# A dual attention kernel: the second batch's rotations ahead of the first score, and the first attention's operands in 64-row halves

## The chip, the cores and the metric

The kernel runs on one core of one Trainium2 chip. A core has a matrix engine (TensorE, PE in the profile; its weight loads are PEld), a vector engine (VectorE, DVE), a scalar engine (ScalarE, ACT), a general engine (GpSimd, POOL) and a queue engine that issues the transfers (SyncE, SP). The metric is the time of one execution on the device, in microseconds; lower is better.

## What is computed

Two sequences of 1024 tokens of width 128 are normalised. The result is the input plus a causal attention plus a small graph of attentions:

```python
xn = layernorm(x)                                  # x: (2, 1024, 128)
# first attention ("A"): 16 heads of width 8, rotated, causal
q, k, v = split(xn @ qkv_w.T + qkv_b)
q, k = apply_rope(q, cos, sin), apply_rope(k, cos, sin)
a = softmax(where(causal, -max, q @ k.T / sqrt(8))) @ v @ out_w.T + out_b
# second attention ("B"): six nodes c, 8 heads of width 16 each, no mask
q = ew[c,0] * (nodes[in_q] @ We[eq] + be[eq])      # k, v alike
nodes[c] = act_w[c] * mha(q, k, v, Wq[c], Wk[c], Wv[c], Wo[c]) + q
out = x + a + layernorm(nodes[5])
```

So there are 32 heads of the first attention (16 for each sequence) and 96 of the second.

## The kernel before

**The work of a head.** A head of either attention has two score products. The first (queries as rows, into the PSUM tiles `s1`, two of 1024 columns) serves only to find each query's largest score, which VectorE takes. GpSimd splits the negated maxima into three bf16 parts (`mparts`), TensorE transposes them into `misc`, ScalarE copies them to `mrows`, and a DMA puts them as three more rows under the queries (`qs`). The second product (keys as rows, into `s2`, two tiles of 512 columns) then has scores less maxima; ScalarE takes the exponential into `probs`, and TensorE multiplies with the values (`vs`) into `cps`. Scores are exact to float32, because queries and keys are split into bf16 parts that DRAM holds as six groups of rows: 6 x 8 = 48 rows in the first attention, 6 x 16 = 96 in the second.

**Operands.** There is a ring of four buffers `qs0..3` and `ks0..3`, 128 rows by 1024. A head of the first attention fills 48 of 96 rows, and the rest are zeros written at the start. The rows 96 to 98 hold the maxima in `qs` and ones in `ks`. First scores read 96 rows, second scores 99. A head's slot is `k % 4`.

**Strips.** Every score product and values' product is cut in four matmuls of 32 output rows each, at `tile_position=(0, c0)` with c0 = 0, 32, 64, 96 (`mm_strips`, and `context` for the values). On the diagonal a product of an identity with `mask_k` adds the causal mask.

**Order.** The work runs in phases of eight heads: `A0`, two of `AL`, `AZ` (the first attention), `B0`, ten of `BL`, `BE` (the second) and a tail `T`. A phase has eight steps k; step k does the first scores of head k, the second scores of head k-2 and the last of head k-3. A step of the first attention has five turns, in each of which TensorE does, in this order: a piece of second scores of head k-2 (up to 512 columns) and its mask; the first scores of head k (1024 columns, 512 in the last turn); the other piece; the values' product of the turn before; in turn 1 the transpose of the maxima; and side work named in a table (`START_AT` for A0, `PREP_A_AT` for AZ). SyncE issues in its own order: the loads of the next head, the raw context of head k-3, the maxima of head k-1, and where there are any the parts of the next operands. In step 7 the loads stand just ahead of the maxima.

**The rotations.** Queries and keys of the first attention come from `rotate` (a 512-column float32 product at full width on TensorE) and `turn` (two products with cosine and sine on VectorE, and for each pair a sum into `full`). ScalarE casts the high part (`high_part`), GpSimd subtracts it (`rest`), ScalarE casts the middle part (`middle_part`), GpSimd subtracts again (`low_part`), and SyncE writes the three parts to DRAM (`write_a`). Rotations 0 to 7 are the first sequence, ahead of the first score; 8 to 15, the second sequence, are side work of the phase A0, at the places marked "rot" in `START_AT`. Between the two stand weight products (`products`, read by ScalarE), the values of the first sequence and 18 one-column bias products (`biases(0)`).

## Time and profile before

| | us |
|---|---|
| median of 3 runs | 1427.39 (1426.09 to 1428.78) |
| the profiled execution | 1423.05 |
| its span | 1421.3 |
| 38.6 to 104.5: phase A0 | 65.9 |
| 104.5 to 208.9: the two phases AL | 104.4 |
| 208.9 to 268.1: phase AZ | 59.2 |
| 268.1 to 1367.7: the second attention | 1099.6 |
| 1367.7 to the end | 53.6 |

A row of a timeline gives start and duration in us, the engine, the line of the program, the operation, the tiles written and read, the shapes (96*32 is 96 rows by 32 columns of weights), the count, and in brackets the idle time before it with what ended it. Rows of one kind that follow each other are merged. A matmul's duration includes its way through the array, so a row's end lies after the start of the next; lengths of TensorE's work are read from start to start. A float32 product counts as two passes.

### The profile page before, as it was taken

What the parts mean: (1) busy time and instruction counts of PE and PEld (TensorE: products, weight loads), DVE (VectorE), ACT (ScalarE), POOL (GpSimd) and SP (SyncE); (2) the same over time, 40 slices, a digit from 0 to 9 for tenths busy, and PEclk for the clock granted to TensorE, in tenths of its full rate; (3) what the DMA queues carried; (4) which work ended last, traced back from release to release, by engine and by line L of the source; (5) the groups of instructions that cost most, each with busy time, mean ns of one, the idle gap of its engine ahead of it and who ended that gap; (6) DMA issues with size and microseconds to landing.
All of it is one profiled execution on the core that took longest, in us unless ns stands there. A gap on an engine that the chain in (4) does not pass through costs nothing.

```text
span 1421.3 us, 60282 instructions
## 1 busy us (share of the span) xinstructions
PE 1380.5 (97%) x26216; PEld 935.3 (66%) x26216; DVE 1263.0 (89%) x1587; ACT 1139.5 (80%) x2133; POOL 449.8 (32%) x936
## 2 busy tenths in 40 slices
PE   6899999999999999999999999999999999999995
PEld 4467777656667666676676766766667666667652
DVE  8889999999989989899899898988989989989895
ACT  3378887688878878888788887887888878878784
POOL 5141115324422433233423332234233432330210
PEclk9899999999999999999999999999999999999998
DMA  8131112343232422333323323233233332321211
GB/s 253 47 116 60 51 59 98 119 142 119 81 127 70 132 97 77 102 109 107 104 78 114 107 74 121 83 123 107 69 101 107 101 107 80 127 98 56 76 38 40
DMA packets 115668, 137.68 MB, mean 97 GB/s; under 512 B 14972, under 2 KB 90109, under 8 KB 115277
## 3 DMA queue, kind: packets, MB, share of 16 engines
q1 hardware_dynamic: 115405, 133.83, 28.7%
q8 instruction: 207, 3.39, 1.0%
q14 instruction: 56, 0.46, 0.1%
HBM read 64.63 MB, written 61.98 MB: 89 GB/s over the span
## 4 chain that ended last, share of the span: by engine, by line
PE 88%; DMA 4%; DVE 3%; SPq 2%; ACT 1%; POOL 1%; issue 1%; ACTq 0%; POOLq 0%; DVEq 0%
PE s L1069 53%; PE cps L1163 26%; PE misc L1069 7%; DMA qs<-mrows 2%; DVE neg_max L971 1%; SPq L431 1%; PE misc L1064 1%; ACT probs L784 1%; DMA dram_raw_b<-csb 1%; PE s L1064 0%; DVE s L967 0%; POOL parts L601 0%; POOL ks L596 0%; POOL full L614 0%; SPq L500 0%
## 5 line engine op out<-in xcount | busy, mean ns | idle before, releaser
L784 ACT ACTIVATE probs<-s 128x512 f32<-128x512 f32 x1792 | 1059.2, 599 | 227.4 <-PE s L1069 166.8
L971 DVE TENSOR_REDUCE neg_max<-s 128x1 f32<-128x1024 f32 x768 | 936.5, 1222 | 62.0 <-PE s L1069 9.1
L1069 PE MATMUL s<-qs,ks 99*32 99x512 bf16 (+2 forms) x7680 | 808.4, 370 | 7.1 <-DMA qs<-mrows 5.1
L1069 PE MATMUL s<-ks,qs 96*32 96x512 bf16 (+2 forms) x7680 | 606.5, 369 | 6.3 <-DMA ks<-dram_qk_a 2.7
L1163 PE MATMUL cps<-probs,vs 128*32 128x256 f32 (+1 forms) x7552 | 591.4, 368 | 0.6 <-ACT probs L784 0.6
L1069 PEld LDWEIGHTS s<-qs,ks 99*32 99x32 bf16 x7680 | 235.8, 94 | 240.6 <-ACT probs L784 96.7
L1163 PEld LDWEIGHTS cps<-probs,vs 128*32 128x32 f32 x7552 | 316.4, 110 | 76.3 <-issue 17.0
L1069 PEld LDWEIGHTS s<-ks,qs 96*32 96x32 bf16 x7680 | 292.5, 97 | 88.6 <-issue 24.5
L633 POOL TENSOR_TENSOR mparts<-neg_max,zeros 128x8 bf16<-128x8 f32 x128 | 26.0, 203 | 796.0 <-DVE neg_max L971 654.3
L967 DVE CUSTOM_DVE_ANT_0 s<-s,mask_q 128x1024 f32<-128x1024 f32 (+7 forms) x256 | 187.8, 785 | 23.5 <-PE s L1069 14.8
L706 POOL TENSOR_TENSOR parts<-full,zeros 128x512 bf16<-128x512 f32 x48 | 61.4, 1280 | 52.2 <-DVE full L949 52.2
L1069 PE MATMUL misc<-srcT,cur 128*32 128x512 f32 x544 | 74.1, 592 | 0.0
L1069 PE MATMUL s<-mask_k,ident_h 128*32 128x128 bf16 x1024 | 65.4, 221 | 0.0
L710 POOL TENSOR_TENSOR parts<-full,zeros 128x512 bf16<-128x512 f32 x48 | 61.4, 1279 | 3.8
L712 POOL TENSOR_TENSOR parts<-full,parts 128x512 bf16<-128x512 f32 x48 | 56.0, 1167 | 3.8
L708 POOL TENSOR_TENSOR full<-full,parts 128x512 f32<-128x512 f32 x48 | 55.9, 1165 | 3.8
L949 DVE TENSOR_SCALAR full<-misc,cur_bias 128x512 f32<-128x512 f32 x48 | 36.0, 750 | 14.0 <-PE misc L1069 12.3
L793 ACT COPY csb<-cps 128x256 f32<-128x256 f32 x128 | 46.9, 367 | 0.8 <-PE cps L1163 0.8
L772 ACT COPY mrows<-misc 24x128 bf16<-24x128 bf16 x128 | 32.4, 253 | 13.3 <-PE misc L1336 13.3
L1069 PEld LDWEIGHTS s<-mask_k,ident_h 128*32 128x32 bf16 x1024 | 33.7, 97 | 4.3 <-issue 1.8
L967 DVE DVE_READ_ACCUMULATOR2_ANT neg_max<- 128x1 f32 x256 | 36.0, 141 | 0.0
L944 DVE TENSOR_SCALAR srcT<-misc,cur_bias 128x512 f32<-128x512 f32 x20 | 15.0, 750 | 23.4 <-PE misc L1069 23.4
(134 smaller groups left out, 607.6 us busy)
## 6 DMA issues: line engine op xcount, KB each, us to landing
dram_qk_b<-parts SPq DMA_DIRECT2D x48, 384.0 KB, 3.2
qs<-dram_qk_b SPq DMA_DIRECT2D x96, 192.0 KB
ks<-dram_qk_b SPq DMA_DIRECT2D x96, 192.0 KB
dram_qk_b<-parts SPq DMA_DIRECT2D x48, 256.0 KB, 3.2
dram_raw_b<-csb SPq DMA_DIRECT2D x93, 128.0 KB, 4.3
dram_qk_b<-parts SPq DMA_DIRECT2D x48, 128.0 KB, 3.2
vsrc<-srcT SPq DMA_DIRECT2D x12, 512.0 KB, 3.1
ctx_b<-dram_raw_b SPq DMA_DIRECT2D x44, 128.0 KB
```

What stands on the lines that cost most here:

```text
L706: pl.tensor_tensor(p[:, 0, :], f[:, :], zeros[:, :], ALU.add).then_inc(parts_done, 1)
L708: pl.tensor_tensor(f[:, :], f[:, :], p[:, 0, :], ALU.subtract).then_inc(parts_done, 1)
L710: pl.tensor_tensor(p[:, 1, :], f[:, :], zeros[:, :], ALU.add).then_inc(parts_done, 1)
L712: pl.tensor_tensor(p[:, 2, :], f[:, :], p[:, 1, :], ALU.subtract).then_inc(parts_done, 1)
L772: nc.scalar.copy(mrows[(k - 1) % 2][:, :], misc_rows).then_inc(mrow_sb, 1)
L784: nc.scalar.activation(buf[:, lo:hi], s2[bank][:, 0:hi - lo], ACT.Exp, scale=scale).then_inc(exp_done, 1)
L793: nc.scalar.copy(csb[(k - 3) % 2][:, :], cps[:, 0:GQ]).then_inc(ctx_sb, 1)
L949: ve.tensor_scalar(full[(2 * (what == "q") + w) % STAGES][:, :], misc[:, :], cur_bias[:, op:op + 1], None, ALU.add).then_inc(prep_full, 1)
L967: last = ve.tensor_tensor_reduce(out=scores, in0=scores, in1=mask_q[:, S - hi + lo:S], scale=-1.0, scalar=-MASKED, op0=ALU.add, op1=ALU.mi ...
L971: last = ve.tensor_reduce(peak, scores, AX.X, ALU.max, negate=True)
L1069: last = te.matmul(dst[c0:c0 + STRIP, :], lhsT[:, c0:c0 + STRIP], rhs, start=start, stop=stop, tile_position=(0, c0))
L1163: last = te.matmul(cps[g * VW:(g + 1) * VW, GQ - 128 * len(mine):GQ], vs[k % RING][:, j, :], blocks[:, first:first + (len(mine) - 1) * ste ...
```

## The change

The rotations 8 to 15 move from the phase A0 to the stretch ahead of the first score. So do their casts on ScalarE; GpSimd's part follows in steps 0 and 1 of A0. The twelve scalings of output and edge weights move from VectorE to ScalarE. The 18 bias products move the other way, behind first scores, in three pieces ("edge"). The side work left in A0 moves to earlier or other turns.

The operands of the first attention lie in two buffers `qa0`, `qa1` (new) and two `ka0`, `ka1` (in the space of `ctx_b`, named so below). Head k uses buffer k % 2, in rows 0 to 63 or 64 to 127 by k % 4 // 2: 48 rows of data and the three rows of maxima or ones behind them. The matmuls of both score products get `tile_position=(row, c0)` with row 0 or 64. The mask is cut to 64 rows too; where a strip's keys lie in the other half, a shifted mask (`mask_far`) stands for `mask_k`. Zero rows are no longer written; GpSimd writes the ones of the second attention's `ks` ahead of its first power. In step 7 of AZ the maxima go ahead of the loads.

```diff
-            (0, 4): ("rot", 8), (1, 2): ("rot", 9), (1, 4): ("rot", 10), (2, 2): ("rot", 11),
...
+START_AT = {(0, 0): ("edge", 0), (0, 1): ("edge", 1), (0, 2): ("edge", 2), (1, 2): ("bias", 1), (1, 4): ("bias", 2),
+            (2, 2): ("bias", 3), (2, 4): ("va", 2), (3, 2): ("va", 3)}
...
+        def first_row(which, k):
+            return HALF_ROWS * (k % RING // 2) if which == "A" else 0
+        def operands(which, k):
+            return (qa[k % 2], ka[k % 2]) if which == "A" else (qs[k % RING], ks[k % RING])
+        def data_rows(which, k):
+            row = first_row(which, k)
+            return slice(row, row + (ROWS_A if which == "A" else KROW))
+        def score_rows(which, k):
+            row = first_row(which, k)
+            return slice(row, row + (ROWS_A if which == "A" else KROW) + 3)
...
-                    if k == UP - 1 and kind not in ("BE", "T"):
+                    if k == UP - 1 and kind not in ("AZ", "BE", "T"):
                         load_unit(kind, r, UP, b)
...
+                    if kind == "AZ" and k == UP - 1:
+                        load_unit(kind, r, UP, b)
...
-                    if kind == "A0" and 2 <= k < 2 + 2 * NCH:
-                        n = 2 * NCH + k - 2
-                        rest(n)
-                        low_part(n)
+                    if kind == "A0" and k == 0:
+                        rest(2 * NCH)
+                        for n in range(2 * NCH + 1, 4 * NCH):
+                            rest(n)
+                            if n < 4 * NCH - 1:
+                                low_part(n - 1)
+                    if kind == "A0" and k == 1:
+                        low_part(4 * NCH - 2)
+                        low_part(4 * NCH - 1)
...
+            for n in range(2 * NCH, 4 * NCH):
+                for h in range(2):
+                    turn(2 * n + h, (s2[0], s2[1], cps, misc)[(2 * n + h) % 4])
...
+            def mask_strips(dst, row):
+                rows = slice(row, row + HALF_ROWS)
+                for c0 in range(0, 128, STRIP):
+                    here = c0 // HALF_ROWS == row // HALF_ROWS
+                    at, mask = (c0, mask_k) if here else ((c0 + HALF_ROWS) % 128, mask_far[row // HALF_ROWS])
+                    last = te.matmul(dst[c0:c0 + STRIP, :], ident_h[rows, at:at + STRIP], mask[rows, :],
+                                     start=False, stop=True, tile_position=(row, c0))
...
-                    last = mm_strips(bank[:, first - lo:end - lo], ky[0:KALL, t * 128:(t + 1) * 128],
-                                     q[0:KALL, q0 + first - at:q0 + end - at], stop=not diagonal)
+                    last = mm_strips(bank[:, first - lo:end - lo], ky[rows, t * 128:(t + 1) * 128],
+                                     q[rows, q0 + first - at:q0 + end - at], stop=not diagonal, row=row)
                     if diagonal:
-                        last = mm_strips(bank[:, at - lo:at - lo + 128], ident_h[:, :], mask_k[:, :],
-                                         start=False)
+                        last = mask_strips(bank[:, at - lo:at - lo + 128], row)
```

TensorE, the end of the stretch ahead of the first score, before (`srcT,w_a` 128x512 is a rotation, `s_0<-srcT` and `s_1<-srcT` are weight products, `be_sb` the bias products, `ks,qs` the first scores):

```order
L1064 MATMUL misc<-be_sb,srcT 128x1 [waits rot_done]
L1064 MATMUL misc<-be_sb,srcT 128x1 x17
L1064 MATMUL s_1<-srcT 128x128 [waits va_sb]
L1064 MATMUL s_1<-srcT 128x128 x2
L1064 MATMUL s_1<-srcT 128x128 [waits va_sb]
L1064 MATMUL s_1<-srcT 128x128 x2
L1064 MATMUL s_0<-srcT 128x128 [waits comp_sb,va_sb]
L1064 MATMUL s_0<-srcT 128x128 x2
L1064 MATMUL s_0<-srcT 128x128 [waits comp_sb,va_sb]
L1064 MATMUL s_0<-srcT 128x128 x2
L1069 MATMUL s_0<-ks,qs 32x512 [waits qk_in0,pool_const,comp_sb]
```

TensorE, the same place now:

```order
L1106 MATMUL s_0<-srcT,w_a 128x512 [waits rot_done,xt_sb]
L1106 MATMUL s_1<-srcT 128x128 [waits va_sb]
L1106 MATMUL s_1<-srcT 128x128 x2
L1106 MATMUL s_1<-srcT,w_a 128x512 [waits rot_done,xt_sb]
L1106 MATMUL s_1<-srcT 128x128 [waits va_sb]
L1106 MATMUL s_1<-srcT 128x128 x2
L1106 MATMUL cps<-srcT,w_a 128x512 [waits rot_done,xt_sb]
L1106 MATMUL s_0<-srcT 128x128 [waits comp_sb,va_sb]
L1106 MATMUL s_0<-srcT 128x128 x2
L1106 MATMUL misc<-srcT,w_a 128x512 [waits rot_done,xt_sb]
L1106 MATMUL s_0<-srcT 128x128 [waits comp_sb,va_sb]
L1106 MATMUL s_0<-srcT 128x128 x2
```

The last four of the eight rotations now stand between the weight products, and the bias products are gone from here.

GpSimd, from the first head's values (`vs`) on, before (L633 to L639 split the maxima of head 0; L614 is `rest`, L601 `low_part`):

```order
L653 COPY vs<-vtok_a 128x8x8 [waits va_sb]
L633 TENSOR_TENSOR mparts<-neg_max,zeros 128x8 [waits max_done]
L635 TENSOR_TENSOR mres<-neg_max,mparts 128x8 [waits max_parts]
L637 TENSOR_TENSOR mparts<-mres,zeros 128x8 [waits max_parts]
L639 TENSOR_TENSOR mparts<-mres,mparts 128x8 [waits max_parts]
L653 COPY vs<-vtok_a 128x8x8
```

GpSimd, the same place now (L647 is `rest`, L634 `low_part`, L666 the first of the split):

```order
L686 COPY vs<-vtok_a 128x8x8 [waits va_sb]
L647 TENSOR_TENSOR full<-full,parts 128x512 [waits rope_hi] x2
L634 TENSOR_TENSOR parts<-full,parts 128x512 [waits rope_mid]
L647 TENSOR_TENSOR full<-full,parts 128x512 [waits rope_hi]
L634 TENSOR_TENSOR parts<-full,parts 128x512 [waits rope_mid]
L647 TENSOR_TENSOR full<-full,parts 128x512 [waits rope_hi]
L666 TENSOR_TENSOR mparts<-neg_max,zeros 128x8 [waits max_done]
```

Six operations of the second sequence now stand ahead of the split of head 0's maxima.

SyncE, the last step of AZ, before (`csb` is the raw context, `mrows` the maxima, `dram_qk_b` the second attention's first operands):

```order
L500 DMA dram_raw_a<-csb0 128x256 [waits ctx_sb]
L431 DMA qs0<-dram_qk_b 96x1x1024 [waits written]
L431 DMA ks0<-dram_qk_b 96x1x1024
L520 DMA qs2<-mrows0 3x8x128 [waits mrow_sb]
L431 DMA qs1<-dram_qk_b 96x1x1024 [waits pv_done]
```

SyncE, the same place now:

```order
L525 DMA dram_raw_a<-csb0 128x256 [waits ctx_sb]
L546 DMA qa0<-mrows0 3x8x128 [waits mrow_sb]
L456 DMA qs0<-dram_qk_b 96x1x1024 [waits written]
L456 DMA ks0<-dram_qk_b 96x1x1024
L456 DMA qs1<-dram_qk_b 96x1x1024 [waits pv_done]
```

The maxima changed places with the two loads.

## Rows read from the trace of the kernel before

**Rows 1.** The page, part 1: busy us, share of the span and instructions by engine.

```profile
PE 1380.5 (97%) x26216; PEld 935.3 (66%) x26216; DVE 1263.0 (89%) x1587; ACT 1139.5 (80%) x2133; POOL 449.8 (32%) x936
```

**Rows 2.** Windows by stage; columns: stretch, length, busy us by engine, TensorE clock, DMA.

```profile
38.60:104.50 65.90, 62.77 (x1239) 38.15 (x1243) 56.64 (x143) 37.73 (x77) 21.80 (x49) 0.92 0.25 82
104.50:208.90 104.40, 104.30 (x2904) 79.76 (x2900) 96.75 (x256) 89.88 (x177) 15.48 (x79) 1.00 0.18 55
208.90:268.10 59.20, 57.50 (x1552) 42.99 (x1548) 52.54 (x135) 44.93 (x89) 28.09 (x60) 1.00 0.34 114
268.10:287.70 19.60, 18.58 (x419) 10.69 (x414) 19.54 (x18) 11.72 (x23) 5.94 (x9) 1.00 0.30 97
```

**Rows 3.** Timeline, VectorE: first tile of heads 1 and 3; columns: start, us, instruction, idle before.

```profile
38.65 1.23 DVE L967 CUSTOM_DVE_ANT_0 s<-s,mask_q 128x1024 f32<-128x1024 f32 x1 [6.11 <-PE s L1069]
...
56.62 1.22 DVE L967 CUSTOM_DVE_ANT_0 s<-s,mask_q 128x1024 f32<-128x1024 f32 x1
```

**Rows 4.** Timeline, TensorE, the head that begins on it at 155.75 us.

```profile
155.75 0.40 PE L1069 MATMUL s<-qs,ks 99*32 99x512 bf16 x4
...
158.40 0.44 PE L1069 MATMUL s<-qs,ks 99*32 99x512 bf16 x4
...
158.68 0.66 PE L1069 MATMUL s<-ks,qs 96*32 96x512 bf16 x12
...
159.40 0.66 PE L1163 MATMUL cps<-probs,vs 128*32 128x256 f32 x10
159.82 0.44 PE L1069 MATMUL s<-qs,ks 99*32 99x512 bf16 x4
...
162.22 0.41 PE L1069 MATMUL s<-qs,ks 99*32 99x512 bf16 x4
```

**Rows 5.** Timeline, VectorE, the same head, first tile at 156.80 us.

```profile
156.80 1.23 DVE L967 CUSTOM_DVE_ANT_0 s<-s,mask_q 128x1024 f32<-128x1024 f32 x1 [0.69 <-POOL mres L635]
...
159.40 0.97 DVE L967 CUSTOM_DVE_ANT_0 s<-s,mask_q 128x768 f32<-128x768 f32 x1
...
162.74 0.14 DVE L967 DVE_READ_ACCUMULATOR2_ANT neg_max<- 128x1 f32 x1
```

**Rows 6.** Timeline, SyncE, then the chain of 150 to 157 us: DMAs of row maxima.

```profile
159.20 0.77 SPq L520 DMA_DIRECT2D qs<-mrows  x1
...
153.12 2.58 DMA qs<-mrows
```

**Rows 7.** Timeline, TensorE: two passes at full width, two in strips, and what follows each.

```profile
59.41 1.12 PE L1064 MATMUL misc<-srcT,w_a 128*128 128x512 f32 x2
60.47 0.40 PE L1069 MATMUL s<-qs,ks 99*32 99x512 bf16 x4
...
1385.52 1.03 PE L1069 MATMUL s<-srcT,comp 128*32 128x512 f32 x8
1386.38 0.39 PE L1069 MATMUL s<-qs,ks 99*32 99x512 bf16 x4
```

**Rows 8.** Timeline, TensorE, around one transpose.

```profile
709.60 0.39 PE L1069 MATMUL s<-qs,ks 99*32 99x512 bf16 x3
709.65 0.22 PE L1336 MATMUL misc<-ident_h,mparts 128*24 128x128 bf16 x1
```

**Rows 9.** Timeline, TensorE, at the end of the first attention.

```profile
267.07 0.40 PE L1069 MATMUL s<-qs,ks 99*32 99x512 bf16 x4 [1.70 <-DMA qs<-mrows]
```

**Rows 10.** Groups by line, 38.6 to 104.5 us: the rotations in the first phase.

```profile
L864 DVE SCALAR_TENSOR_TENSOR rope<-misc,bias_a,table 128x512 f32<-128x512 f32 x8 | 6.0, 748 | 1.1 <-PE misc L1064 0.7
...
L870 DVE TENSOR_TENSOR full<-rope 128x512 f32<-128x512 f32 x4 | 2.8, 694 | 0.1
```

**Rows 11.** Timeline, prologue: GpSimd, TensorE, ScalarE.

```profile
15.39 3.98 POOL L596 MEMSET ks<- 32x1024 bf16 x4
...
26.17 4.08 PE L1064 MATMUL misc<-be_sb,srcT 128*128 128x1 f32 x36
...
35.22 0.88 ACT L741 ACTIVATE comp<-s,ewb 128x128 f32<-128x128 f32 x3 [0.35 <-PE s L1064]
```

More of the change, by code:

```diff
@@ L1106, in _ @@
             pe.wait_ge(wqk_in, 16)
-            for m in range(4 * NCH):
+            for m in range(8 * NCH):
                 pe.wait_ge(xt_sb, m // 4 + 1)
@@ L1277, in score_piece @@
                 which = kind_at(kind, k, 2)
-                q, ky = qs[(k - 2) % RING], ks[(k - 2) % RING]
+                q, ky = operands(which, k - 2)
+                rows, row = score_rows(which, k - 2), first_row(which, k - 2)
                 lo, hi = pieces(which, j)[n]
```

141 lines of the change are left out of this document (78 added, 63 removed).

## The prediction

> **What bounds the kernel now.** I read the page first: TensorE is busy for 97% of the span, VectorE for 89% [rows 1]. The busy time by stage comes next: the first attention fills three windows (its first phase, two phases without side work, a last phase that also prepares the second attention), 229.5 us of 1421.3, and only these windows are touched by the change, with the prologue ahead of them [rows 2]. In the middle window TensorE is busy for 104.30 of 104.40 us and VectorE for 96.75. The windows begin where VectorE takes a head's first 1024-wide tile: head 1 at 38.65, head 3 at 56.62 [rows 3], head 9 at 104.5. The 16 heads of the middle window take 6.52 us each, and eight heads cost 65.9 us in the first window and 59.2 in the last.
>
> One head on TensorE, start to start [rows 4]: a turn begins with one score piece and its diagonal mask, 0.28 (158.40 to 158.68); the tile's first scores and the second piece with its mask take 0.72, the probabilities times values 0.42, together 1.42. By columns (512, 128; 1024; 512, 128) the 1.00 of scores is 0.22 + 0.06, 0.44, and 0.22 + 0.06. Three such turns leave 2.2 us of the head's 6.47 (155.75 to 162.22) for the shorter first and last. Nothing is idle, so **TensorE is the bound**. VectorE is close behind: its last read of a head starts 5.94 us after its first tile, with no gap marked before the tiles but for short waits on the next scores, two a head, as before the tile at 159.40 [rows 5]. I estimate 0.3 us for them from the starts and durations, and 5.65 us for a head without them. A third loop runs through SyncE: the DMA that brings the row maxima back is issued 2.40 us after the head's first tile (159.20 against 156.80 [rows 5, 6]), lands about 2.6 us later, and TensorE needs 0.8 to 1.1 us from there to the next head's first tile (some 0.7 us of scores and 0.36 until VectorE starts). That loop is 5.8 to 6.1 us. So a faster TensorE can bring a head from 6.5 to about 5.9, not further.
>
> **Part 1: half-height operands.** Both score products of the first attention go from 96 and 99 rows to 48 and 51, in rows 0 to 63 or 64 to 127. Head k's first scores and head k-2's second scores always lie in opposite halves. The count of matmuls and columns is unchanged: a mask is still one per strip. The height alone buys nothing: 99-row and 96-row pieces take their 0.22 us for 512 columns alike [rows 4].
>
> What it can buy is overlap of the halves. Per turn the second scores are 0.22 + 0.06 + 0.22 + 0.06 = 0.56 and the first 0.44; side by side they take 0.56 instead of 1.00. No row shows two halves at work. The nearest is the column strips: four matmuls of 512 columns cost 0.22, the price of one. And strips do not wait for each other: the transpose is ahead of the next scores in the program and uses the first strip only; it starts at 709.65, while three of the four scores behind it had started at 709.60 [rows 8]. One strip was late and the others passed it. I take it that the halves behave alike.
>
> What it costs: the values' product keeps all 128 rows, so the array's division changes twice a turn, ten times a head. No row shows 64 against 128 rows. The nearest change is 32-column strips to full width: two passes of 512 columns cost 0.86 in strips (1385.52 to 1386.38) and 1.06 at full width between strips (59.41 to 60.47) [rows 7]. That is 0.20 for two changes, 0.10 each, with whatever part of it is weight loading. Bounds 0 and 0.2; I take 0.10, the measured one.
> The Trainium skill, page "TensorEngine Tiling (Array Packing)", section "Key Properties", says that changing the tiling mode drains the engine, and that different tiles can run in parallel. The first speaks against this change and agrees with the 0.10; the second no run here shows.
>
> TensorE per head follows. Full overlap: three turns 0.56 + 0.42 + 0.20 = 1.18, first turn about 1.0, last turn 0.28 + 0.42 + 0.20 = 0.90, sum **5.45**. If starts keep program order over the halves, the second piece can begin only when the first scores' last group has begun: a turn is 0.22 + 0.22 + 0.28 + 0.42 + 0.20 = 1.34, the head **6.2 to 6.3**. No overlap at all: 6.47 + 10 x 0.10 = **7.5**. The page "TensorE: Matmul & The Clock Gate", section "The mechanism", of the Trainium skill has matmuls start and end strictly in program order; rows 8 disagree for strips, and by that rule the time would be the middle value's.
>
> Middle window, full overlap: VectorE and the maxima loop set 5.9. The eighth head of a phase has its loads ahead of the maxima DMA (the one of 153.12 in rows 6, by my estimate 0.7 us later in its head than the other), which keeps 6.5. 14 x 5.9 + 2 x 6.5 = 95.6 against 104.4: **-8.8**. In program order 14 x 6.35 + 2 x 6.8 = 102.5: -1.9. Serial 16 x 7.5 = 120: +15.6.
>
> Last window (59.2 us): four heads carry one projection, two strip passes, together 0.86 on TensorE as in rows 7, and SyncE's writes; I put them at 6.7 against some 7.35, the seventh with two at 7.3. In the eighth the maxima DMA now goes ahead of the loads for the second attention. Before, it went behind them, and TensorE sat 1.70 us for it until 267.07 [rows 9]. Now it lands early, but the loads start about 1.4 us later and the first tile of the second attention waits for them: I put this head at 9.2 against 8.3. Sum 5.9 x 2 + 6.7 x 4 + 7.3 + 9.2 = 55.1: **-4.1**. In program order about 0, serial +8.
>
> Where the first two heads of the second attention share turns with the last two of the first, each turn of the old kind now changes the division up to four times: 2 x 18 x 0.10 = 3.6 us on TensorE. In that stretch VectorE is busy for 19.54 of 19.60 us and TensorE for 18.58 [rows 2], so about 1 us of the 3.6 is covered. Some more is in turns without a piece of the first attention. I take **+2.0**; bounds 0 and 3.6.
>
> **Part 2: the second batch's rotations.** Before, eight of them sit in the first phase: eight products on TensorE, 8 x 0.748 + 4 x 0.694 = 8.8 us on VectorE [rows 10]. Each stands in a turn at full width (1.06 us with its two changes [rows 7]). Now they stand ahead of the first score. What hides them there: TensorE spent 4.08 us on 36 passes of one-column bias products (now behind the first scores in three pieces); VectorE sat idle 6.11 us before the first tile [rows 3, 11]. The way of the operands to DRAM and back is not longer, since GpSimd's four memsets (3.98 us), which held its first subtraction until 19.4, now stand ahead of its first power [rows 11]. But TensorE gets 8 x 0.86 = 6.9 us [rows 7] less 4.1: up to +2.8 on its way to the last weight product, which ScalarE copied out by 36.1 [rows 11]. The first score waits for that copy as for its operands, and had 1.8 us of room. I leave the first tile at 38.6, bounds 37 and 40.5.
>
> Behind it stands the cost of the move. ScalarE now does 12 activations taken from VectorE (0.29 each by the three of 0.88 us in rows 11, 3.5 us), then eight casts; GpSimd does rest, rest, low, rest, low, rest, six of about 1.2 us, in program order **ahead of** head 0's maxima, and TensorE's transpose waits for these. From 38 + 3.5 + 0.6: 42.1 + 7.0 = 49.1, split maxima at about 50, transposed and copied at 50.6, DMA to 53.2 [rows 6], the third head's first tile not before 54.3; I take 54.8 against 56.62: **-1.8**. Heads 3 to 8 took 47.9 us. They lose five rotations, keep two value products and one bias, and keep SyncE's write of three parts behind each load: 7.2 + 6.9 + 3 x 6.8 + 6.7 = 41.2: **-6.7**. In program order 42.5, serial 47.7.
>
> **Sum.** -1.8 - 6.7 - 8.8 - 4.1 + 2.0 = -19.4. The profiled execution took 1423.05 us (span 1421.3), the median is 1427.39, 4.3 above it. I carry the difference over: 1427.4 - 19.4 = **1408.0**.
>
> **Rivals.**
> Starts in program order across the halves: -1.8 - 5.4 - 1.9 + 0 + 2.0 = -7.1, 1420. For it: no row shows halves; against it: rows 8.
> The halves do not run side by side and each division change costs 0.10: -1.8 - 0.2 + 15.6 + 8 + 2.0 = +23.6, **1451**, slower. It decides where the values' product meets the scores, ten times a head. With some 30 heads and 6 to 8 us from part 2, the kernel is slower once TensorE's head goes above about 6.7 us, that is when overlap saves less than 0.8 of the 1.0 us that the changes cost. Against it: strips show that parts of the array work side by side.
> Overlap works but a change costs about 0.2: TensorE's head is 6.5 and only part 2 is left: about 1423.
> The rotations are only displaced (the first tile comes at 41, the third head later still): 1408 + 5 = 1413; inside the range.
>
> **How the numbers follow.** Full overlap (with the displaced rotations) 0.52, program order 0.22, dear changes 0.10, serial 0.16. The forecast is the first. The range reaches from 1398 (loop at 5.65, first tile at 37) to 1429 and leaves the serial case out. A measurement here tells 0.2% (2.9 us) from no change. Faster: 0.52 + 0.22 + half of dear = 0.78; same 0.04; slower 0.18.
>
> **What would show it.** Middle window 104.4 to about 96 us with VectorE busy near its whole length; first and second scores with starts inside each other's 0.2 us; ten gaps of 0.1 us a head around the values' product; third head's first tile near 55; the window from 287.7 to 1367.7 (the second attention after its first heads) unchanged in length. A middle window of 120 us would prove me wrong on overlap, one of 102 on order, and a first tile after 41 on the prologue.

## The result: slower by 0.5% where 1.4% faster was forecast

| kernel | median, us | lowest to highest | runs |
|---|---|---|---|
| before | 1428.40 | 1426.09 to 1431.25 | 10 |
| after | 1434.27 | 1432.96 to 1441.12 | 10 |

The ratio is 1.0054, 95% interval 1.0042 to 1.0066: 6 to 9 us lost. The forecast was 1408.0 in a range of 1398 to 1429, so even the range missed. The profiled execution of the changed kernel has a span of 1431.6 us against 1421.3. Times and ratios here are of executions whose mean granted clock is 0.97 or more; two of the four of x4, at 0.87, took 1627 and 1635 us and stand in none of them.

The page, part 1 and the granted TensorE clock by slice:

```profile
PE 1385.3 (97%) x26216; PEld 878.2 (61%) x26216; DVE 1256.8 (88%) x1569; ACT 1136.3 (79%) x2145; POOL 450.9 (31%) x940
...
PEclk9699999799999999999999999999999999999998
```

Beside [rows 1] no share of a working engine has moved by more than a point; only the weight loads fell, from 66% to 61%. So the page's first part does not show where the time went. The clock line does: the second slice (36 to 72 us) and the eighth (251 to 286 us) stand at 6 and 7, where the page of the kernel before has 8 and 9. The windows by stage, to be laid beside [rows 2]; columns: stretch, length, busy us by engine, clock, DMA share, GB/s:

```profile
36.70:57.80 21.10, 18.97 (x170) 12.02 (x173) 13.86 (x37) 7.50 (x19) 10.39 (x16) 0.54 0.06 21
57.80:104.20 46.40, 44.21 (x1104) 22.48 (x1088) 36.41 (x98) 32.56 (x67) 11.04 (x34) 0.88 0.32 107
104.20:206.60 102.40, 98.41 (x2904) 50.53 (x2896) 94.65 (x256) 84.58 (x177) 16.02 (x83) 1.00 0.19 56
206.60:265.50 58.90, 54.41 (x1544) 27.72 (x1536) 51.65 (x134) 42.63 (x89) 27.49 (x57) 0.98 0.35 115
265.50:282.40 16.90, 16.90 (x205) 5.60 (x204) 9.75 (x9) 6.00 (x11) 0.00 (x0) 0.55 0.10 32
282.40:294.30 11.90, 11.56 (x222) 4.88 (x221) 10.69 (x11) 5.90 (x12) 5.90 (x9) 1.00 0.35 113
```

| stretch | before | after | forecast change | measured change |
|---|---|---|---|---|
| to the third head's first tile | 56.62 | 57.80 | -1.8 | +1.2 |
| heads 3 to 8 | 47.9 | 46.4 | -6.7 | -1.5 |
| middle window, 16 heads | 104.4 | 102.4 | -8.8 | -2.0 |
| last window, 8 heads | 59.2 | 58.9 | -4.1 | -0.3 |
| first two heads of the second attention | 19.6 | 28.8 | +2.0 | +9.2 |

Together +6.6. The other 3.7 us of the longer span lie behind them, in heads whose instructions are the same: from VectorE's first tile of the third of these heads to its last they took 1089.1 us before and 1093.2 after, and 1089.1 to 1098.5 over the profiles of this study, whatever had been changed. I take that stretch for one execution's scatter: the profiled execution was 5.4 us faster than its kernel's median before, and 0.8 after. From here on kernels are compared by the time at which that third head begins (287.7 before, 294.3 after), and by the ratio of their runs. The first of these measures scatters too. Four kernels that are the same up to the eighth head of the last phase (after, x1, x2, x14) begin it at 253.9 to 255.8 us, so less than 2 us there says nothing.

Where the +9.2 comes from stands in the timeline of TensorE, VectorE and SyncE at the end of the first attention; columns: start, us, instruction, and in brackets the idle time ahead of it:

```profile
257.64 0.76 SPq L546 DMA_DIRECT2D qa<-mrows  x1
258.44 0.81 SPq L456 DMA_DIRECT2D qs<-dram_qk_b  x1
259.29 0.75 SPq L456 DMA_DIRECT2D ks<-dram_qk_b  x1
...
264.34 1.04 PE L1111 MATMUL s<-ks,qs 96*32 96x512 bf16 x8 [3.04 <-DMA ks<-dram_qk_b]
...
265.51 1.22 DVE L1013 TENSOR_REDUCE neg_max<-s 128x1 f32<-128x1024 f32 x1 [4.24 <-PE s L1111]
```

The chain of waits has this load in it; columns: start, us, what:

```profile
259.29 5.01 DMA ks<-dram_qk_b
```

The load of the second attention's operands is issued behind the maxima DMA and TensorE stands idle for 3.04 us. But the stall is not the loss. Eight 512-column strips take 1.04 us behind it, where the same group took 0.60 to 0.65 from 284 us on: the clock is at its lower level of 1.2 GHz, as the windows show, and stays there for 17 us:

```profile
262.00:264.00 2.00, 0.00 (x0) 0.00 (x0) 0.00 (x0) 0.01 (x1) 0.54 (x3) 0.91 0.29 103
264.00:268.00 4.00, 3.66 (x40) 0.97 (x44) 1.82 (x2) 0.97 (x2) 0.00 (x0) 0.50 0.00 0
...
276.00:280.00 4.00, 4.00 (x56) 1.64 (x51) 1.55 (x3) 1.44 (x3) 0.00 (x0) 0.50 0.00 0
280.00:284.00 4.00, 4.00 (x63) 1.46 (x55) 3.84 (x4) 1.46 (x3) 1.04 (x5) 0.91 0.02 4
```

Before the change TensorE sat idle for 1.70 us at the same place [rows 9] and the clock stayed at 1.00.

Side by side work did come. Start times in one turn of the middle window:

```profile
150.43 0.40 PE L1111 MATMUL s<-qa,ctx_b 51*32 51x512 bf16 x4
150.46 0.40 PE L1111 MATMUL s<-ctx_b,qa 48*32 48x512 bf16 x4
...
150.69 0.28 PE L1111 MATMUL s<-ctx_b,qa 48*32 48x256 bf16 x4
150.72 0.28 PE L1111 MATMUL s<-qa,ctx_b 51*32 51x256 bf16 x4
150.80 0.28 PE L1111 MATMUL s<-ctx_b,qa 48*32 48x256 bf16 x4
...
151.09 0.36 PEld L1218 LDWEIGHTS cps<-probs,vs 128*32 128x32 f32 x10 [0.16 <-issue]
151.66 0.10 PEld L1111 LDWEIGHTS s<-qa,ctx_b 51*32 51x32 bf16 x4 [0.21 <-ACT probs L835]
```

A second score (51 rows) and a first score (48 rows) start 0.03 us apart and the next matmuls of each half follow 0.23 us later; and the second piece (150.72) starts ahead of a first score that stands before it in the program (150.80). Weight loads stand still for 0.16 us ahead of the values' product, where they wait for nothing that the profile shows, and for 0.21 us ahead of the next score, which the profile puts down to ScalarE.

### The profile page after: what moved, and what is told of

Same layout as the page of the kernel before. It is cut to its first block, busy times and chain, and to the rows that moved or that the text cites. A ratio compares the mean times of both kernels' runs of the same rounds, so it can differ in the third digit from the quotient of the medians.

```text
span 1431.6 us, 60283 instructions
## 1 busy us (share of the span) xinstructions
PE 1385.3 (97%) x26216; PEld 878.2 (61%) x26216; DVE 1256.8 (88%) x1569; ACT 1136.3 (79%) x2145; POOL 450.9 (31%) x940
## 4 chain that ended last, share of the span: by engine, by line
PE 81%; DMA 8%; SPq 6%; ACT 2%; DVE 2%; issue 1%; POOL 0%; ACTq 0%; DVEq 0%
PE s L1111 46%; PE cps L1218 24%; PE misc L1111 7%; DMA qs<-mrows 3%; DMA dram_raw_b<-csb 2%; SPq L456 2%; ACT probs L835 2%; SPq L493 1%; PE misc L1106 1%; DMA qa<-mrows 1%; SPq L424 1%; PE s L1121 1%; DMA ctx_b<-dram_qk_a 1%; PE s L1106 1%; SPq L502 1%
## 5 line engine op out<-in xcount | busy, mean ns | idle before, releaser
L1111 PE MATMUL s<-qs,ks 99*32 99x512 bf16 x6144 | 684.9, 381 | 6.2 <-DMA qs<-mrows 4.3
L1111 PE MATMUL s<-ks,qs 96*32 96x512 bf16 x6144 | 512.0, 381 | 4.0 <-DMA ks<-dram_qk_b 3.0
L1111 PEld LDWEIGHTS s<-qs,ks 99*32 99x32 bf16 x6144 | 183.4, 93 | 218.9 <-ACT probs L835 88.2
L1111 PEld LDWEIGHTS s<-ks,qs 96*32 96x32 bf16 x6144 | 248.1, 98 | 65.0 <-issue 20.4
L666 POOL TENSOR_TENSOR mparts<-neg_max,zeros 128x8 bf16<-128x8 f32 x128 | 26.0, 203 | 815.8 <-DVE neg_max L1013 666.0
L1111 PE MATMUL s<-qa,ctx_b 51*32 51x512 bf16 (+3 forms) x1536 | 111.2, 341 | 6.4 <-ACT probs L835 4.4
L1111 PE MATMUL s<-ctx_b,qa 48*32 48x512 bf16 (+3 forms) x1536 | 96.2, 344 | 4.7 <-DMA ctx_b<-dram_qk_a 2.5
L1111 PEld LDWEIGHTS s<-qa,ctx_b 51*32 51x32 bf16 x1536 | 31.5, 91 | 66.5 <-ACT probs L835 42.6
L1121 PE MATMUL s<-mask_k,ident_h 64*32 64x128 bf16 x512 | 58.2, 224 | 0.0
L1121 PE MATMUL s<-mask_far,ident_h 64*32 64x128 bf16 x512 | 58.2, 224 | 0.0
```

The costliest lines, as they stand in the source:

```text
L1111: last = te.matmul(dst[c0:c0 + STRIP, :], lhsT[:, c0:c0 + STRIP], rhs, start=start, stop=stop, tile_position=(row, c0))
L1121: last = te.matmul(dst[c0:c0 + STRIP, :], ident_h[rows, at:at + STRIP], mask[rows, :], start=False, stop=True, tile_position=(row, c0))
```

## Experiments

All kernels below start from the changed kernel unless said otherwise. "Third head" is the time at which the third head of the second attention begins. Code cuts are shown in part; `...` marks what is left out.

| kernel | third head, us | median, us | ratio to before, 95% interval |
|---|---|---|---|
| before | 287.7 | 1428.4 | |
| after | 294.3 | 1434.3 | 1.0054, 1.0042 to 1.0066 |
| x1, loads first | 292.2 | 1431.8 | 1.0028, 1.0015 to 1.0041 |
| x2, seven products in the stall | 289.4 | 1429.8 | 1.0007, 0.9995 to 1.0019 |
| x3, rotations only | 287.5 | 1426.5 | 0.9990, 0.9978 to 1.0003 |
| x5, biases early | 295.1 | 1432.7 | 1.0033, 1.0021 to 1.0045 |
| x6, projections early | 297.8 | 1435.7 | 1.0049, 1.0032 to 1.0067 |
| x8, all three | 282.9 | 1422.0 | 0.9961, 0.9948 to 0.9974 |
| x11, x8 and 30 products | 285.3 | 1425.2 | 0.9993, 0.9981 to 1.0005 |
| x12, x8 at full height | 286.5 | 1424.9 | 0.9990, 0.9980 to 1.0000 |
| x13, full height, late loads | 288.9 | 1428.4 | 1.0013, 0.9998 to 1.0028 |
| x14, loads first, one product | 284.6 | 1422.3 | 0.9967, 0.9954 to 0.9980 |
| x15, x8 and 10 products | 290.1 | 1429.1 | 1.0015, 1.0001 to 1.0030 |
| x16, halves only | 293.6 | 1433.2 | 1.0050, 1.0038 to 1.0063 |

### x1: the loads first

```diff
-                    if k == UP - 1 and kind not in ("AZ", "BE", "T"):
+                    if k == UP - 1 and kind not in ("BE", "T"):
                         load_unit(kind, r, UP, b)
...
-                    if kind == "AZ" and k == UP - 1:
-                        load_unit(kind, r, UP, b)
```

> The changed kernel with one thing undone: in the eighth head of the last first-attention phase the loads for the second attention go ahead of the maxima DMA again. Theory 1 (the loads wait for a chain of fixed length: the last projection's parts are written at 253.6 us, land some 4.5 us later, and only then can the load of 5 us begin; the half clock follows from TensorE's idle time): the loads move by 0.8 us at most (258.44 to some 257.7), the maxima DMA goes 1.6 us later and lands behind them, TensorE is still idle for about 3 us, its clock is still halved, the second attention's first head stays at 15 to 17 us and the time within 1.5 us of 1434. Theory 2 (the order on SyncE alone is the cause, as my prediction had it with 9.2 us for that head): TensorE idle as before the change, 1.7 us, no half clock, first head 9 to 10 us, time 1424 to 1427. Theory 3 (four division changes a turn cost the 7 us): head at 16, time 1434 whatever the idle time.

The stall became 1.68 us, now for the maxima, as short as before the change. The clock fell all the same and the first head took 16.1 us. The gain of 2.1 us is that of the eighth head (8.4 us instead of 10.2) and of the first head (16.1 instead of 16.9), less some 0.5 us of scatter ahead of and behind them. Theory 2 falls, and so does the part of theory 1 that wanted 3 us of idle time. The fall is no accident of one execution: the mean granted clock is 0.978 to 0.982 in all twelve of x1 and 0.975 to 0.981 in all ten of the changed kernel, and 0.987 to 0.992 in those of the kernel before. Timeline of TensorE, then windows, of x1:

```profile
263.01 0.40 PE L1109 MATMUL s<-qa,ctx_b 51*32 51x512 bf16 x4 [1.68 <-DMA qa<-mrows]
```
```profile
264.00:268.00 4.00, 4.00 (x60) 1.16 (x56) 3.44 (x3) 1.97 (x5) 0.00 (x0) 0.60 0.21 53
268.00:272.00 4.00, 4.00 (x51) 1.51 (x47) 1.47 (x2) 1.46 (x3) 0.00 (x0) 0.50 0.23 82
```

### x2: products that keep TensorE busy

```diff
+                            if (kind, k, i) == ("B0", 0, 0):
+                                need(pe, mrow_sb, UP * ph - 1)
+                                for f in range(7):
+                                    mm(misc[:, :], w_a[:, f % 2 * D:(f % 2 + 1) * D], srcT[:, f % 2 * CH:(f % 2 + 1) * CH])
```

> The changed kernel with seven extra products of 512 columns (nobody reads their result), queued on TensorE between the last second scores' first piece and the first scores of the second attention, where it stood idle for 3.4 us. Theory 1 (the idle time brought the half clock, and the half clock made the second attention's first head 16.9 us long): the extra products fill some 3 us of the idle time, the granted clock stays at its full level from 264 us on, that head takes 9.1 to 10.5 us, the time falls by 6 to 8 us to 1426 to 1428. Theory 3 (division changes in mixed turns are the cost): the head stays above 14 us and the time at 1434 or more.

I had mis-sized them: each is two passes, and the 14 took 6.28 us, some 3 more than the stall. The time fell nevertheless, by 4.5 us (6 to 8 expected), because the clock stayed up. TensorE's timeline, and the windows of the two heads:

```profile
260.19 6.28 PE L1106 MATMUL misc<-srcT,w_a 128*128 128x512 f32 x14
```
```profile
267.10:277.50 10.40, 10.23 (x205) 4.10 (x201) 9.33 (x8) 5.89 (x11) 0.00 (x0) 1.00 0.17 53
277.50:289.40 11.90, 11.56 (x221) 4.88 (x221) 10.71 (x11) 5.89 (x11) 5.90 (x9) 1.00 0.35 113
```

10.4 and 11.9 us at full clock against 16.9 and 11.9, and 9.1 and 10.5 before: the half clock costs 6.5 us, the divided turns 2.7. Theory 3 holds for those 2.7 only.

### x3 and x16: each half of the change alone

x3 gives the operands their full height back, and puts the loads ahead of the maxima DMA again:

```diff
-            return (qa[k % 2], ka[k % 2]) if which == "A" else (qs[k % RING], ks[k % RING])
+            return qs[k % RING], ks[k % RING]
...
```

> Only the second half of the change: the second batch is rotated ahead of the first score, the operands of the first attention have the full height of before (96 and 99 rows) and the loads stand ahead of the maxima DMA as before. Theory A (the bias products, moved behind the first scores, stand in VectorE's way at half clock and eat what the earlier rotations give): third head's first tile at 57 to 58 us against 56.62, middle window 104.4, last window 59.2, second attention's first head 9.1, time within 2 us of before (1427 to 1430). Theory B (the rotations do give the 8.5 us that I predicted and the division changes at half clock took them again): window from the third head to the middle one 42 us, time 1419 to 1422.

Theory A: 0.9990, third head's first tile of the first attention at 58.3 (37.9 plus 11.5 and 8.8 us), middle heads 6.49, the second attention's first head 9.1. The early rotations alone give 0.1%, which the interval does not tell from nothing.

x16 has the half-height operands with rotations, biases and weight products as before:

```diff
+START_AT = {(0, 0): ("bias", 1), (0, 1): ("bias", 2), (0, 2): ("bias", 3),
+            (0, 4): ("rot", 8), (1, 2): ("rot", 9), (1, 4): ("rot", 10), (2, 2): ("rot", 11),
...
```

> Only the first half of the change: half-height operands, with the second batch's rotations, the bias products and the products of weights where they were before. With the rotations the clock should be back by 50 us as before; middle heads 6.31, last ones 7.06; the loads behind the maxima DMA give the stall of 3 us and the half clock where the second attention begins: 16.9 and 11.9 us for its first two heads. Sum against before: -3.0 in the middle, -2 in the last window, +7.8 +1.4 at the boundary, about +4: 1430 to 1433. If the early rotations were what made the changed kernel slower, it would be at or below 1428.

1.0050, the boundary (the place where the second attention begins) as in the changed kernel: stall 2.81 us, half clock, 17.0 and 12.0 us for the two heads. The loss belongs to the first part of the change. One expectation failed: the clock at the start was back at 61 us and not by 50, although the rotations stood in the turns again. In x3, without them and at full height, it was 61 us too.

### x4: the same half for both scores

```diff
-            return HALF_ROWS * (k % RING // 2) if which == "A" else 0
+            return 0
-            return (qa[k % 2], ka[k % 2]) if which == "A" else (qs[k % RING], ks[k % RING])
+            return qs[k % RING], ks[k % RING]
...
```

> The changed kernel with all operands of the first attention in rows 0 to 63 (48 and 51 rows, in eight tiles of their own), so that first and second scores can't run side by side while the division of the array still changes ten times a head. If the halves do overlap in the changed kernel and a change costs 0.10 us, a head of the middle window takes 7.3 to 7.5 us (against 6.31), the window 117 to 120 us (against 102.4), and the 32 heads together add 30 to 36 us: 1464 to 1470. If overlap brought nothing there (heads bound by order across the halves), the window would stay near 103 and the time near 1434.

A middle head takes 7.60 us, the kernel 1.0311 times the one before (1.0281 to 1.0341), some 1472 us. VectorE's first tiles of two such heads:

```profile
143.57 1.23 DVE L1009 CUSTOM_DVE_ANT_0 s<-s,mask_q 128x1024 f32<-128x1024 f32 x1 [0.74 <-PE s L1111]
151.17 1.23 DVE L1009 CUSTOM_DVE_ANT_0 s<-s,mask_q 128x1024 f32<-128x1024 f32 x1 [0.74 <-PE s L1111]
```

Against 6.50 at full height that is 1.10 for ten changes of the division, 0.11 each: my 0.10 was right, and so was the 7.5 for serial halves. Side by side work takes 1.3 us off a head.

### x7, x9, x10: what sets a middle head at 6.31 us

```diff
+                            skip = 128 if kind[0] == "A" and hi - lo > 128 else 0
+                            lo += skip
...
+                                hi -= 128 if kind == "AL" and hi - lo == CH else 0
```

x7 has the first two lines, on VectorE: it leaves the first 128 keys out of the maxima. x9 has the last one, on ScalarE: it leaves 128 columns of each long piece out of the exponentials, in the two middle phases. x10 has all three. Each was run once; what counts here is the length of a head.

> The changed kernel with VectorE's reads of the first attention's scores 128 columns shorter in all tiles wider than 128 (the first 128 keys are left out of the maxima), seven reads a head, some 0.13 us each: VectorE's work falls from 5.92 to some 5.0 us a head, TensorE's stays. If VectorE's own work and its hand-over of the tiles set the 6.31 us of a middle head, a head falls by 0.4 or more, to 5.9 or less, where the maxima loop takes over. If TensorE sets them (second scores held back by program order, the rival of 6.2 to 6.3), the head stays at 6.2 to 6.3.

> The changed kernel with ScalarE's exponentials 128 columns shorter in every piece of 512 columns in the two middle phases of the first attention (the last 128 columns of such a piece are left out and keep older values). ScalarE's work falls by some 0.13 us for each of its long pieces, VectorE's and TensorE's stay. Shorter VectorE reads alone had left the middle head at 6.31 us. If the round trip between TensorE and ScalarE sets the head (a piece's exponential ends, the product with the values and the next piece and mask follow on TensorE, then ScalarE starts again), the head falls to 5.8 to 6.2 us. If TensorE's own order across the halves sets it (the rival of my prediction), or VectorE and TensorE together, it stays within 0.05 of 6.31.

> Both cuts together: VectorE's reads 128 columns shorter in all of the first attention and ScalarE's exponentials 128 columns shorter in its two middle phases (those columns are left out). If two loops of nearly the same length (VectorE's tiles, and TensorE with ScalarE) each hold the head at 6.31 us, this falls clearly below what the shorter exponentials alone give: 5.5 to 5.9 us. If the TensorE-ScalarE loop alone sets it, it is the same as there. If TensorE's program order sets it: 6.2 to 6.3.

The same tile in two heads that follow each other, of x7, x9 and x10 in turn:

```profile
140.21 1.10 DVE L1011 CUSTOM_DVE_ANT_0 s<-s,mask_q 128x896 f32<-128x896 f32 x1 [0.56 <-POOL mres L668]
146.51 1.10 DVE L1011 CUSTOM_DVE_ANT_0 s<-s,mask_q 128x896 f32<-128x896 f32 x1 [0.56 <-POOL mres L668]
```
```profile
128.00 1.23 DVE L1010 CUSTOM_DVE_ANT_0 s<-s,mask_q 128x1024 f32<-128x1024 f32 x1 [0.27 <-PE s L1112]
134.09 1.23 DVE L1010 CUSTOM_DVE_ANT_0 s<-s,mask_q 128x1024 f32<-128x1024 f32 x1 [0.27 <-PE s L1112]
```
```profile
126.44 1.10 DVE L1012 CUSTOM_DVE_ANT_0 s<-s,mask_q 128x896 f32<-128x896 f32 x1 [0.56 <-POOL mres L668]
132.34 1.10 DVE L1012 CUSTOM_DVE_ANT_0 s<-s,mask_q 128x896 f32<-128x896 f32 x1 [0.56 <-POOL mres L668]
```

6.31 with less VectorE work, 6.10 with less ScalarE work, 5.90 with both. So the round trip of TensorE and ScalarE sets the head, VectorE's tiles stand 0.2 us behind it, and TensorE's program, which is the same in all three, needs 5.90 or less. What sets the 5.90 of x10 is open. The rival "program order, 6.2 to 6.3" had the right number for the wrong reason. The round trip in the changed kernel's ScalarE timeline, one head:

```profile
164.13 2.31 ACT L835 ACTIVATE probs<-s 128x512 f32<-128x512 f32 x4 [0.18 <-PE s L1121]
166.79 0.60 ACT L835 ACTIVATE rec_b<-s 128x512 f32<-128x512 f32 x1 [0.34 <-PE s L1121]
167.74 1.08 ACT L835 ACTIVATE probs<-s 128x512 f32<-128x512 f32 x2 [0.35 <-PE s L1121]
```

Four exponentials run without a gap, while TensorE waits for a bank that ScalarE has read; then TensorE's values' product stands ahead of the next piece and mask, and ScalarE waits 0.34 and 0.35 us. I take it that the two banks for the second scores are too few to cover both; no run has more of them.

### x5, x6, x8: the version that beats both

x5 takes the bias products back ahead of the first score; x6 moves the projections of the last window, and the writes of their parts, one head earlier:

```diff
-START_AT = {(0, 0): ("edge", 0), (0, 1): ("edge", 1), (0, 2): ("edge", 2), (1, 2): ("bias", 1), (1, 4): ("bias", 2),
+START_AT = {(1, 2): ("bias", 1), (1, 4): ("bias", 2),
...
-PREP_A_AT = {(2, 2): ("k", 0), (3, 2): ("k", 1), (4, 2): ("q", 0), (5, 2): ("q", 1),
+PREP_A_AT = {(1, 2): ("k", 0), (2, 2): ("k", 1), (3, 2): ("q", 0), (4, 2): ("q", 1),
...
```

> The changed kernel with the 18 bias products of one column back ahead of the first score (behind the weight products), and VectorE's sums of them too. In the changed kernel they stand in three pieces inside the first head and take 1.43, 2.65 and 2.66 us of TensorE at half clock, and VectorE waits behind each. If these pieces are what ate the gain of the early rotations, the first head takes 7 to 8 us instead of 12.3, the first score comes 1 to 2 us later, and everything up to the middle window comes 3 to 4 us earlier: time 1430 to 1431 against 1434. If the half clock of this stretch is the cause whatever is queued there, the heads behind take up the difference and the time stays within 1.5 us of 1434.

> The changed kernel with the four key and query projections of the last first-attention phase, and the writes of their parts, one head earlier; the loads for the second attention still behind the maxima DMA of the eighth head. Theory 1 (a chain of fixed length from the last projection to the loads sets the stall): the loads no longer wait for the write and are issued at once behind the maxima DMA, but that is the same place on SyncE, 258.4 us by the trace of the changed kernel, so the stall is shortened only by the time that the load itself takes less without the write's traffic (5.0 us to some 3 to 4): idle time 1.5 to 2.5 us, time 1430 to 1434. If the stall comes from the order on SyncE alone, nothing changes: 1434.

x5: first tile at 41.5, first head 6.4 us instead of 12.3: 1.1 us of gain by the end of the first head, 1.6 in the median, but no gain by the third head of the second attention (295.1 against 294.3), so no more than the 1.1 us is shown. Its own third head took 11.6 us at half clock against 9.0, which is not its doing: x1 and x2, the changed kernel up to there, took 12.35. x6: the stall is still 2.75 us (1.5 to 2.5 expected; the load takes 4.7 us with the write gone from beside it), the half clock lasts longer still, two slow heads instead of one (17.8 and 19.3 us): nothing won.

x8 has both, and issues the loads one head earlier, behind the seventh head's maxima DMA:

```diff
-                    if kind == "AZ" and k == UP - 1:
+                    if kind == "AZ" and k == UP - 2:
                         load_unit(kind, r, UP, b)
```

> The changed kernel with the bias products back ahead of the first score, the four projections one head earlier, and the loads for the second attention in the seventh head instead of the eighth, behind its maxima DMA. Then neither operands nor maxima are late where the second attention begins: TensorE idle under 1 us there, clock at its full level, first head of the second attention 10.4 us as with the filler, and 3 us less idle time than there: from the filler's 1429.8 less 3 us of overfilling, less up to 3 us of the biases: 1424 to 1427. If the half clock comes anyway, 1430 or more.

0.9961, better than the 1424 to 1427 us expected: TensorE shows no wait at the boundary, and the clock stays:

```profile
262.00:266.00 4.00, 4.00 (x83) 1.56 (x76) 3.41 (x4) 2.64 (x5) 0.00 (x0) 1.00 0.35 110
266.00:270.00 4.00, 3.88 (x86) 1.67 (x78) 3.55 (x4) 1.80 (x4) 0.00 (x0) 1.00 0.08 27
```

x12 is x8 with operands of full height, which need the loads back in the eighth head, ahead of its maxima DMA:

> The faster version (1422.0 us) with the first attention's operands at full height as before the change, and the loads for the second attention ahead of the maxima DMA in the eighth head, which full-height operands need. It tells what the half-height operands bring once the clock drop where the second attention begins is gone. By the heads: -0.19 us in each of 16 middle heads, -0.3 in each of the last seven, +2.7 us in the two mixed heads, and what a stall of 1.5 us at the boundary costs this one: half-height ahead by 2 to 5 us, this kernel at 1424 to 1427. If the half-height operands bring nothing on the whole: 1421 to 1423.

0.9990. So half height, with the earlier loads that it allows, brings 0.3% (4 us) once the clock stays up, 3.6 us of it by the third head: x8 reaches the second attention 6.2 us earlier (260.6 against 266.8), 1.5 of them a stall that x12 has and x8 has not, and loses 2.6 us in its first two heads (22.3 against 19.7).

### x13 and x14: idle time or kind of work

x13 is x3 with the loads behind the maxima DMA. x14 is x1 and one product of 512 columns, `mm(misc[:, :], w_a[:, 0:D], srcT[:, 0:CH])`, ahead of the wait for the maxima.

> Early rotations and full-height operands, but the loads for the second attention behind the eighth head's maxima DMA, as the changed kernel has them. Its twin with the loads first lost 1.47 us of TensorE there and kept the full clock. If the length of the idle time alone decides, TensorE is idle here for 2.5 to 4 us, the clock falls to half as in the changed kernel and the first head of the second attention takes 14 to 17 us: time 1432 to 1435. If full-height work leaves the clock up even after a stall of this length, the first head takes 9.1 us and only the stall is added: 1427 to 1429.

> The changed kernel with the loads ahead of the maxima DMA (there TensorE was idle for 1.68 us and the clock was halved all the same, 1431.8 us) and one extra product of 512 columns (two passes, 0.9 us, read by nobody) ahead of the wait for the maxima. If the idle time is what halves the clock at half-height operands too, 0.8 us of it leave the clock at its full level: first head of the second attention 10.4 us, second 11.9, time 1425 to 1428. If the clock falls for another reason (the light mixed turns that follow), the head stays at 16 us and the time at 1431 to 1432.

The stall and the clock behind it, x13 and then x14:

```profile
268.51 0.62 PE L1110 MATMUL s<-ks,qs 96*32 96x512 bf16 x8 [2.62 <-DMA ks<-dram_qk_b]
```
```profile
266.00:268.50 2.50, 0.00 (x0) 0.00 (x0) 0.07 (x2) 0.60 (x1) 1.03 (x5) 1.00 0.32 119
268.50:272.00 3.50, 3.23 (x76) 1.77 (x80) 2.75 (x3) 1.98 (x4) 0.00 (x0) 1.00 0.08 19
```
```profile
259.44 1.13 PE L1104 MATMUL misc<-srcT,w_a 128*128 128x512 f32 x2
261.14 0.40 PE L1109 MATMUL s<-qa,ctx_b 51*32 51x512 bf16 x4 [0.57 <-DMA qa<-mrows]
```
```profile
262.00:266.00 4.00, 4.00 (x77) 1.32 (x73) 3.48 (x3) 2.72 (x6) 0.00 (x0) 1.00 0.19 53
```

At full height 2.62 us of idle time leave the clock up. At half height 1.68 us halve it (x1) and 0.57 us, after one product at full width, don't. So the length of the stall doesn't decide alone; which of the two things that x14 has changed, less idle time or a product at full width, kept the clock up isn't separated. Every execution agrees: mean clock 0.986 to 0.988 in the ten of x13, 0.987 and 0.988 in the four of x14. One product of 1.1 us that nobody reads goes with 0.9967 instead of 1.0028, 8.7 us. Not all of that is its doing: the traces show 5.7 us in the first two heads (22.3 against 28.1), and 1.8 us that x14's profiled execution was ahead of x1's before it reached the product.

### x11 and x15: buying the clock back in the first heads

```diff
+                        if kind == "A0" and (k, i) in [(0, 0), (0, 1), (0, 2), (0, 3), (0, 4), (1, 0), (1, 1), (1, 2), (1, 3), (1, 4)]:
+                            for f in range(3):
+                                mm(cps[:, GQ:2 * GQ], w_a[:, f % 2 * D:(f % 2 + 1) * D], srcT[:, f % 2 * GQ:(f % 2 + 1) * GQ])
```

That is x11, which starts from x8 and has these products behind ten turns, three each; x15 has two each, behind the five turns of the first head.

> The faster version (biases and projections early, loads in the seventh head; 1422.0 us) with three extra products of 256 columns at full width, read by nobody, behind each of the ten turns of the first two heads. There TensorE's clock is at half from 40 to 66 us; before the change it was back at its full level at 49 us, with eight rotations in the heads. If it is TensorE's lighter work in these heads (products of one column, half-height scores, no rotations) that holds the clock down, the clock comes back by 50 to 55 us, the third and fourth head fall from 11.8 and 7.8 us towards 8 and 7 and the time by 2 to 4 us, to 1418 to 1420. If the clock doesn't come back sooner, the extra products cost up to 0.7 us a turn at half clock: 1424 to 1429.

> The faster version (1422.0 us) with two extra products of 256 columns behind each of the five turns of the first head alone, where TensorE waits 0.3 to 1.4 us for VectorE (3.1 us in sum), instead of three behind each of ten turns. If a third of the extra work already brings the clock back by 50 us without standing in VectorE's way, the heads 2 to 4 shrink from 8.8, 11.8 and 7.8 us by 3 to 5 us in sum against up to 2 us in the first: 1419 to 1421. If not, it costs what stands in the way: 1422 to 1425.

x11 has its clock back at 43 us, where x8 waits until 67. But the first two heads pay 7.1 us for it and the next ones give 4.2 back: 0.9993 against 0.9961, where I had expected 1418 to 1420 us. x15 paid 6.6 us in the first head and its clock came back at 76 only: 1.0015. From 50 us on, windows of x11 and of x8:

```profile
50.00:58.00 8.00, 8.00 (x65) 5.42 (x63) 4.55 (x12) 0.26 (x1) 3.20 (x7) 1.00 0.08 21
```
```profile
50.00:58.00 8.00, 7.99 (x90) 4.33 (x90) 5.43 (x17) 1.87 (x4) 1.57 (x6) 0.50 0.10 27
```

How much work of which kind brings the clock back is open. It also differs between executions of the same instructions: the changed kernel and x6 had it back at 62 us, x1 and x2 at 70.

## Why the prediction was wrong, by its own steps

**Middle heads, 5.9 us forecast, 6.31 measured.** TensorE's sum was sound: changes 0.11 each, serial 7.60, and 5.90 or less with side by side halves (5.45 forecast; no run came nearer to it than 5.9). The loops beside it were mis-sized. I named VectorE (5.65) and the maxima (5.8 to 6.1), and left out ScalarE, though [rows 2] show it busy for 89.88 of 104.40 us, 5.6 a head. Its round trip with TensorE takes 6.31; VectorE's loop 6.10, where I had taken off waits that come back with every tile. The Trainium skill, page "TensorEngine Tiling (Array Packing)", section "Performance Considerations", says that the copy out of PSUM may become the bottleneck after a 4x speedup of TensorE. Here it did after a far smaller one: shorter reads took 0.21 us (x9) and 0.41 us (x10) off a head. This step cost 6.8 of the 8.8 us of the middle window and most of the last one's.

**Order across the halves.** The rows at 150.72 and 150.80 show a piece in one half pass a score in the other. My reading of [rows 8] carried over. The Trainium skill, page "TensorE: Matmul & The Clock Gate", section "The mechanism", has starts in program order; this trace does not agree.

**The eighth head and the boundary, 9.2 us and +2.0 forecast.** The head took 10.2: the load was issued 4.0 us after its first tile (255.34) and landed 5.0 us later. I had moved the loads by the 1.4 us of their place on SyncE and not worked out when they land. The divided turns cost 2.7 at full clock, inside my bounds of 0 to 3.6. What failed is that the sum has no term for the clock: it costs these heads at the full clock of [rows 2], which had held through the stall of 1.70 us in [rows 9]. I had forecast a longer head and did not ask what the clock would do at its wait. That is the term that changed the sign: 6.5 us of half clock.

**Heads 1 to 8, -8.5 forecast, -0.3 measured.** The first tile came 2.0 us earlier. Then the bias products, which I had as hidden, stood inside the first head, at half clock. The group of line L1106, 36.4 to 44.4 us; columns: ns of one (least, median, most), first and last start, form:

```profile
L1106 PE MATMUL misc<-be_sb,srcT x36: 250/352/371, 36.4 to 44.4; 128*128 128x1 f32 x36
```

The same 36 passes had taken 4.08 us in the prologue [rows 11]. In heads 3 to 8 the larger part is the clock again. Before, it was back at 49 us; in the changed kernel at 62, and I costed these heads at full clock, 41.2 us. Two kernels that are still the changed one here show its price, x6 and then x1:

```profile
62.00:66.00 4.00, 4.00 (x85) 2.58 (x80) 2.88 (x11) 1.68 (x3) 0.38 (x2) 0.94 0.00 0
```
```profile
62.00:66.00 4.00, 4.00 (x64) 1.99 (x60) 2.74 (x9) 1.54 (x3) 0.00 (x0) 0.50 0.01 2
```

x6, back at 62, took 42.8 us for heads 3 to 8; x1, back at 70, took 46.3. The changed kernel was back at 62, but its profile has a second drop at 82 to 90 us, behind 1.05 us of waiting for a load, which no other profile shows, and took 46.4. Why the clock came back later than before isn't known: x16 and x3, each with one half of the change, were both at 61.

**Rivals.** The serial one fell by rows and by x4. "Program order" gave the nearest time for the middle and last windows (-1.9 and 0), but not its cause. None of my cases held the half clock. The range left out the serial case and had nothing else above the time of before, so it ended at 1429. The chances of a faster kernel add up to 0.79, not 0.78.

## What to carry to other kernels

When a change makes one engine's work lighter or opens a stall on TensorE, look at the granted clock on both sides of every stall and cost the work behind it at both levels; here that was worth more than the change itself. Before crediting a faster engine, write down the round trip with each engine that reads its result, ScalarE included, and take the longest. And where an idle wait on TensorE can't be removed, one product into a free bank is worth trying: x14 ran 0.6% faster than x1 with it, and some 0.4% of that shows in the trace where the clock stayed up.

## What was not expected of the hardware

- The clock fell after 1.68 us of idle time behind half-height work (x1) and stayed after 2.62 us behind full-height work (x13), in every execution of either by its mean clock.
- Once down it stayed down for 17 us (264 to 281), although TensorE then waited little. In x6 it lasted from 261 to some 293 us.
- Matmuls in the two row halves run truly side by side: 0.03 us between starts, 0.22 us for both, 1.3 us off a head of 7.6.
- Fewer active rows bought nothing by themselves: 51-row and 48-row groups of 512 columns took the 0.22 us of 99 rows.
